# Two fused transformer layers on one core: loads of the first layer regrouped, the second layer's first weights loaded during the first layer's last batch, merged mask products and new step tables

## What is computed

```python
x = L0_attn_x                                     # [16, 512, 128]
xn = _layernorm(x)
x = x + attn0(xn) + soft_moe(xn)
xn = _layernorm(x)
x = x + attn1(xn) + routed_moe(xn)
# attn0: 16 heads; q = xn @ W_q (8 a head), c_kv = xn @ W_kv_down, k, v = c_kv @ W_k_up, c_kv @ W_v_up (8 a head),
#        one rotary part of 32 for all heads, causal softmax, @ W_o
# soft_moe: slots normed by rms, logits = norm(xn) . slots; softmax over tokens (dispatch) and over the
#        8*64 slots (combine); per expert gelu(slots @ w1 + b1) @ w2 + b2
# attn1: 16 heads of 64, keys and values from a latent of 128, causal softmax, @ w_out
# routed_moe: sigmoid scores of 16 experts, the top 8 by score + bias, normed and scaled;
#        silu(x w_gate) * (x w_up), w_down, and one shared expert
```

## Time and profile before

| | value |
|---|---|
| median of 3 runs | 3098.85 us (3097.3 to 3101.01) |
| the profiled execution | 3096.49 us, span 3094.8 us |
| mean granted PE clock | 0.984 |
| PE busy | 2884.3 us (93%) in 23492 matmuls |
| DVE / ACT / POOL busy | 2310.2 (75%) / 1802.6 (58%) / 1314.4 (42%) us |

### The profile page before, as it was taken

How to read it: one execution, slowest core, us unless ns; L and a number is a source line. 1 busy time by engine, 2 the same in 40 slices (tenths; PEclk the granted TensorE clock), 3 DMA queues, 4 the chain that set the end, 5 groups by cost and what they waited for, 6 DMA issues and landing times.

```text
span 3094.8 us, 63911 instructions
## 1 busy us (share of the span) xinstructions
PE 2884.3 (93%) x23492; PEld 1512.2 (49%) x23492; DVE 2310.2 (75%) x4199; ACT 1802.6 (58%) x3771; POOL 1314.4 (42%) x1223
## 2 busy tenths in 40 slices
PE   3999999999999984999999999999999999999997
PEld 1555555555555551444444444444444444444443
DVE  4777777777777755778878878878778778778874
ACT  2777766667776763555555555555555555555543
POOL 0433333333333321544544554554554554544543
PEclk8999999999999996999999999999999999999998
DMA  4222222222222214444444444444444444444442
GB/s 112 59 57 54 53 72 68 54 59 56 59 52 61 68 29 131 117 119 115 120 122 116 120 122 115 121 121 115 123 119 116 122 120 115 126 117 115 118 120 69
DMA packets 271910, 297.70 MB, mean 96 GB/s; under 512 B 30832, under 2 KB 235760, under 8 KB 271088
## 3 DMA queue, kind: packets, MB, share of 16 engines
q1 hardware_dynamic: 249936, 276.88, 35.2%
q10 hardware_dynamic: 21664, 16.73, 1.7%
HBM read 141.46 MB, written 25.69 MB: 54 GB/s over the span
## 4 chain that ended last, share of the span: by engine, by line
PE 51%; DMA 3%; DVE 3%; issue 2%; SPq 2%; ACT 1%; POOL 0%; DVEq 0%; ACTq 0%; POOLq 0%
PE l_ps_out L1643 8%; PE l_ps_any L1543 6%; PE l_ps_any L1545 6%; PE l_ps_any L1544 6%; PE l_ps_any L1668 5%; PE l_ps_exp L1626 4%; PE l_ps_any L1675 4%; PE l_ps_exp L1628 4%; PE l_ps_any L1601 3%; DMA l_y_rec<-rec_scratch 2%; PE l_ps_sum L1654 2%; PE l_ps_exp L1630 2%; SPq L1173 1%; DVE l_neg_max L1466 1%; PE l_ps_any L1606 1%
## 5 line engine op out<-in xcount | busy, mean ns | idle before, releaser
L1260 POOL TENSOR_TENSOR l_hid<-l_hid,l_spread 128x512 f32<-128x512 f32 x256 | 327.9, 1281 | 655.1 <-DVE l_hid L1495 480.3
L1347 ACT ACTIVATE l_probs<-l_ps_exp 128x512 f32<-128x512 f32 x640 | 376.8, 595 | 211.4 <-PE l_ps_exp L1630 201.0
L673 DVE TENSOR_REDUCE neg_max<-ps_any 128x1 f32<-128x384 f32 (+3 forms) x704 | 411.0, 634 | 115.7 <-PE ps_any L800 113.7
L536 ACT ACTIVATE probs<-ps_exp 128x512 f32<-128x512 f32 x640 | 352.1, 607 | 41.5 <-PE ps_exp L815 28.4
L455 POOL TENSOR_SCALAR_AFFINE_SELECT probs<-probs 128x512 f32<-128x512 f32 x256 | 160.0, 637 | 458.9 <-ACT probs L536 457.4
L1466 DVE TENSOR_REDUCE l_neg_max<-l_ps_any 128x2 f32<-128x768 f32 (+2 forms) x384 | 316.1, 862 | 35.4 <-PE l_ps_any L1606 34.4
L1626 PE MATMUL l_ps_exp<-l_q_a,l_k_a 128*128 128x512 f16 (+3 forms) x1024 | 306.4, 300 | 10.3 <-DMA l_q_b<-l_max_row 6.5
L1643 PE MATMUL l_ps_out<-l_probs,l_v 128*64 128x512 f32 (+3 forms) x2048 | 303.9, 439 | 0.7 <-ACT l_yT L1322 0.7
L1499 DVE TENSOR_TENSOR l_hw<-l_hid,l_hw 128x512 f16<-128x512 f32 x272 | 257.9, 953 | 60.2 <-ACT l_hw L1330 60.0
L1353 ACT ACTIVATE l_hid<-l_ps_any 128x512 f32<-128x512 f32 x272 | 162.4, 597 | 236.3 <-PE l_ps_any L1545 217.9
L1628 PE MATMUL l_ps_exp<-l_q_b,l_k_b 65*128 65x512 f16 (+3 forms) x1024 | 295.2, 300 | 0.0
(11 more groups left out here) (262 smaller groups left out, 6731.5 us busy)
## 6 DMA issues: line engine op xcount, KB each, us to landing
l_spread<-route_scratch SPq DMA_DIRECT2D x128, 512.0 KB, 4.7
l_q_a<-l_q_hi SPq DMA_DIRECT2D x256, 128.0 KB, 2.4
l_y_rec<-rec_scratch SPq DMA_DIRECT2D x128, 256.0 KB, 4.3
l_q_b<-l_q_lo SPq DMA_DIRECT2D x128, 128.0 KB, 2.4
l_k_a<-l_k_hi SPq DMA_DIRECT2D x128, 128.0 KB, 3.2
l_k_a<-l_k_lo SPq DMA_DIRECT2D x128, 128.0 KB, 2.8
l_k_b<-l_k_hi SPq DMA_DIRECT2D x128, 128.0 KB, 2.9
q_st<-rot_hi SPq DMA_DIRECT2D x64, 128.0 KB
```

The costliest lines, as they stand in the source:

```text
L536: nc.scalar.activation(probs[:, n % 2, u], ps_exp[:, (10 * g + u) % 3], ACT.Exp, scale=float(HD0 + DR) ** -0.5).then_inc(exp_done.sem, 1)
L673: nc.vector.tensor_reduce(neg_max[:, n % 2, heads[0]:heads[0] + k, t], src, AX.X, ALU.max, negate=True).then_inc(drained["dve"], 1)
L1260: nc.gpsimd.tensor_tensor(at, at, spread[:, c % 3, n % SPREAD], ALU.mult).then_inc(weighted.sem, 1)
L1347: nc.scalar.activation(probs[:, n % 2, u], ps_exp[:, (5 * p + u) % ST_BANKS], ACT.Exp, scale=float(HD1) ** -0.5).then_inc(exp_done.sem, 1)
```

## The change

Seven things are changed.

1. x of batch 0 is SP's first DMA. Of the 18 loads 8 stay with SP; the six of the rotary weights, `gamma`, the slot embeddings, `slot_gamma` and `w_o` go to ACT, ahead of w1, b1 and w2; the eight b2 go to SP, behind `load_heads(0, 2)`.
2. The norm of the slots becomes a step `snT` of the program, eight steps ahead of the first logits. The casts of the masks follow the first `scale`; `v_aug` is cleared by POOL instead of DVE.
3. A class `Early` keeps buffers that both layers share. Fourteen loads of layer 1 (masks, w_kv_down, gate, bias, w_q, w_kv_up, w_gate) are issued by ACT, one before each exponential of the last 14 of batch 15. SP loads layer 1's first x after `load_heads(15, 3)`.
4. ACT no longer waits for the last store; layer 1's loads of x wait for their own batch's.
5. At the start of layer 1, DVE norms x first and then makes the low parts, w_g's ahead of the route; w_u and w_d are cast just ahead of the first expert product and the first `hw`. PE waits for one weight at a time.
6. The mask products of a unit are merged: one of `exp` for all blocks (640 in place of 1024), one for each half and side of `max` (1280 in place of 2048).
7. Both tables are written anew, with the same steps in another order.

```diff
-    ("exp", 0, 0, 4), ("logits_s", 0, 0), ("exp", 0, 0, 5), ("exp", 0, 0, 6), ("soft_s", 0, 0),
...
+    ("exp", 0, 0, 1), ("attnT", -1, 0), ("exp", 0, 0, 2), ("max", 0, 1, 5), ("exp", 0, 0, 3), ("max", 0, 1, 6),
...
-    return [x for x in steps if 0 <= x[1] < batches]
+    steps = [x for x in steps if 0 <= x[1] < batches]
+    first = min(steps.index(x) for x in (("logits_s", 0, 0), ("logits_c", 0, 0)))
+    return steps[:first - 8] + [("snT", 0, 0)] + steps[first - 8:]
...
+        loads = [(ident[:], a["ident"]), (w_kvd[:], a["L0_attn_W_kv_down"]), (w_q[:], a["L0_attn_W_q"]),
+                 (w_k[:], a["L0_attn_W_k_up"]), (cos[:], a["cos"]), (sin[:], a["sin"]), (w_v[:], a["L0_attn_W_v_up"]),
+                 (mask[:], a["mask"])]
+        act_loads = rope + [
+            (gamma[:], a["L0_ffn_norm_gamma"].partition_broadcast(P)),
+            (slot_nat[:], a["L0_ffn_slot_embeds"].rearrange("e s d -> (e s) d").rearrange("(m p) d -> p m d", p=P)),
+            (slot_gamma[:], a["L0_ffn_slot_norm_gamma"].partition_broadcast(P)), (w_o[:], a["L0_attn_W_o"])]
...
+            sp.dma_start(x_in[:], a["L0_attn_x"][0].rearrange("(t p) d -> p t d", p=P)).then_inc(x_loaded.sem, 16)
             for dst, src in loads:
                 sp.dma_start(dst, src).then_inc(loaded, 16)
...
+                if name == "load_heads" and (b, n) == (0, 2):
+                    for dst, src in b2_loads:
+                        sp.dma_start(dst, src).then_inc(late_loaded, 16)
+                if name == "load_heads" and (b, n) == (batches - 1, G - 1):
+                    sp.wait_ge(stored.sem, stored.at(0, 16))
+                    sp.dma_start(early.x_in[:], x1_dram[0].rearrange("(t p) d -> p t d", p=P)
+                                 ).then_inc(early.x_loaded.sem, 16)
...
+            nc.gpsimd.memset(v_aug[:], 0.0).then_inc(prep_pool, 1)
+            pool.wait_ge(prep_pool, 2)
+            nc.gpsimd.memset(v_aug[:, :, :, HD0:HD0 + 1], 1.0).then_inc(prep_pool, 1)
...
+            for dst, src in act_loads:
+                act.dma_start(dst, src).then_inc(act_loaded, 16)
             act.dma_start(w1_in, a["L0_ffn_w1"].rearrange("e d h -> d e h")).then_inc(w1_loaded, 16)
             for dst, src in late_loads:
                 act.dma_start(dst, src).then_inc(late_loaded, 16)
-            act.wait_ge(prep_pe, 1)
-            nc.scalar.activation(snT[:, 0], ps_any[:, 0], ACT.Copy).then_inc(prep_act, 1)
-            act.wait_ge(prep, 13)
-            act.wait_ge(loaded, all_loaded)
...
                     act.wait_ge(exp_full.sem, exp_full.at(g, u + 1))
+                    k = len(early.loads) - (G - n) * len(EXP0) + u if b == batches - 1 else -1
+                    if k >= 0:
+                        act.dma_start(*early.loads[k]).then_inc(early.loaded, 16)
                     nc.scalar.activation(probs[:, n % 2, u], ps_exp[:, (10 * g + u) % 3], ACT.Exp,
                                          scale=float(HD0 + DR) ** -0.5).then_inc(exp_done.sem, 1)
...
                     act.dma_start(x1_dram[b].rearrange("(t p) d -> p t d", p=P), x1[:]).then_inc(stored.sem, 16)
-            act.wait_ge(stored.sem, stored.at(batches, 0))
...
-    ("v", 0, 2, 0), ("rec", -1, 1), ("sums", -1, 7), ("exp", 0, 0, 4), ("v", 0, 3, 0), ("exp", 0, 1, 0),
...
+    ("exp", 0, 0, 4), ("max", 0, 1, 2), ("exp", 0, 1, 0), ("exp", 0, 1, 1), ("v", 0, 2, 0), ("v", 0, 3, 0),
...
+            high_weights(split_in[:4])
...
                 if at == first_expert:
-                    act.wait_ge(late_loaded, all_late)
-                    for w, src in split_late:
-                        nc.scalar.activation(w[:, 0], src, ACT.Copy, scale=W_SCALE).then_inc(weights_hi, 1)
-                    act.wait_ge(weights_lo, len(split_in) + len(split_late))
+                    act.wait_ge(up_loaded, 32)
+                    high_weights(split_late[:1])
+                if at == first_hw:
+                    act.wait_ge(down_loaded, 32)
+                    high_weights(split_late[1:])
+                    act.wait_ge(weights_lo, len(split_in) + 1)
+                if name == "xnT" and b == 0:
+                    high_weights(split_in[4:])
+                if name == "exp" and (b, n, step[3]) == (0, 0, 0):
+                    act.wait_ge(weights_lo, len(split_in))
...
-            low_weights(split_in, 0)
...
                 if at == first_expert:
-                    low_weights(split_late, len(split_in))
+                    low_weights(split_late[:1], len(split_in))
+                if at == first_hw:
+                    low_weights(split_late[1:], len(split_in) + 1)
...
+                if name == "scale" and b == 0:
+                    dve.wait_ge(early.loaded, early.all)
+                    low_weights(split_in[:3], 0)
                 if name == "scale":
                     dve.wait_ge(rstd_ok.sem, rstd_ok.at(b, 1))
                     nc.vector.scalar_tensor_tensor(out=shift[:], in0=mv[:, :, 0], scalar=-1.0, in1=rstd[:],
                                                    op0=ALU.mult, op1=ALU.mult).then_inc(stats_ok.sem, 1)
+                if name == "xnT" and b == 0:
+                    low_weights(split_in[3:4], 3)
+                    casts()
+                if name == "gate" and b == 0:
+                    low_weights(split_in[4:], 4)
...
                 if at == first_expert:
-                    pe.wait_ge(weights_lo, len(split_in) + len(split_late))
-                    pe.wait_ge(late_loaded, all_late)
+                    pe.wait_ge(weights_lo, len(split_in))
+                if name == "up_in" and step[1:] == (0, 0):
+                    pe.wait_ge(weights_lo, len(split_in) + 1)
+                if name == "down" and step[1:] == (0, 0):
+                    pe.wait_ge(weights_lo, len(split_in) + 2)
...
+                if name == "max" and step[1:] == (0, 0, 0):
+                    pe.wait_ge(prep, 14)
+                    pe.wait_ge(prep_pool, 2)
+                    pe.wait_ge(weights_lo, len(split_in))
...
-                    for q, t, c in MAX1[step[3]]:
+                    for k, (q, t, c) in enumerate(MAX1[step[3]]):
                         w = (t + 1) * P
                         for r, rows in sides:
                             pe.matmul(scores[r][:, c:c + w], q_hi[rows, q, t * P:t * P + P], k_hi[rows, q, 0:w],
-                                      start=True, stop=False)
-                        for half in range(2):
-                            to = c + t * P + HD1 * half
-                            for r, rows in sides:
-                                ins = pe.matmul(scores[r][:, to:to + HD1], later_h[rows, half], ident_2[rows],
-                                                start=False, stop=(half == 1))
+                                      start=(k == 0), stop=False)
+                    blocks = diagonals([c + t * P for q, t, c in MAX1[step[3]]])
+                    for half in range(2):
+                        for r in range(2):
+                            rows = slice(HD1 * r, HD1 * r + HD1)
+                            out = scores[r].rearrange("p (x h k) -> p x h k", h=2, k=HD1)[:, blocks, half]
+                            ins = pe.matmul(out, later_h[rows, half], ident_2[rows, 0:len(MAX1[step[3]])],
+                                            start=False, stop=(half == 1))
...
-                                  start=True, stop=False)
+                                  start=(c == 0), stop=False)
-                        ins = pe.matmul(out[:, 0:P], ident_h[:], mask_h[:], start=False, stop=True)
-                    ins.then_inc(exp_full.sem, 1)
+                    out = ps_exp[:, m % ST_BANKS].rearrange("p (x q) -> p x q", q=P)
+                    pe.matmul(out[:, diagonals([c for r, k, c in EXP1[step[3]]])], ident_h[:],
+                              mask_h[:, 0:len(EXP1[step[3]])], start=False, stop=True
+                              ).then_inc(exp_full.sem, 1)
...
+class Early:
+        self.stage = ctx.enter_context(nc.sbuf_tensor("stage", [P, STAGE], F32))
+        self.ident = ctx.enter_context(nc.sbuf_tensor("ident", [P, P], F32))
+        self.bias = ctx.enter_context(nc.sbuf_tensor("l1_bias", [P, E1], F32))
+        self.loaded = ctx.enter_context(nc.semaphore("early_loaded"))
+        self.x_in = ctx.enter_context(nc.sbuf_tensor("l1_x_in", [P, TB, D], F32))
+        self.x_loaded = Count(ctx, nc, "l1_x_loaded", 16)
+        self.stored = Count(ctx, nc, "l0_stored", 16)
+        self.loads = [(masks[HD1 * r:HD1 * r + HD1, half], a["maskT"][HD1 * half:HD1 * half + HD1])
+                      for r in range(2) for half in range(2)]
+        self.loads += [(masks[:, 2], a["maskT"]), (w_kvd, a["L1_attn_w_kv_down"]), (gate, a["L1_ffn_gate_w"]),
+                       (self.bias[:], a["L1_ffn_expert_bias"].partition_broadcast(P)), (w_q, a["L1_attn_w_q"])]
+        self.loads += [(w_kvu[:, k:k + H * HD1], of[:, k:k + H * HD1]) for k in (0, H * HD1)]
+        of = a["L1_ffn_w_gate"]
```

(26 more changed lines are left out.)

334 lines of the change are left out of this document (171 added, 163 removed).

## The result

The changed kernel takes 3156.57 us (median of 4 runs, 3151.89 to 3161.88) against 3098.76 us: a ratio of 1.0186, 95% interval 1.0169 to 1.0204. It is 58 us slower where 46 us less were forecast.

A forecast was written before the change was run, and what follows sets the result against it. PE's own work was taken to bound both layers, leaving its idle time to win. -13 - 18.1 - 18.7 + 3.3 = -46.5 on 3096.5 gives 3050; the runs' median, 2.4 us above, gives 3052, range 3024 to 3080.

The forecast's parts named there:

- The start, -13: Start of layer 0: x loaded first lets PE begin sooner, first score product at 28 to 34 us; -13 us (8 to 19).
- 22 - 3.5 = 18.5: Start: ACT's copy of `xnT` 22 us earlier, less 3.5 for q and k's way through DRAM while w1 and w2 arrive.
- The slots' wait: Start: PE waits in full at `snT` for the slots' norm, some 5.5 us given back.
- The crossing, -18: From layer 0 to layer 1: PE's first instruction comes 21.1 us earlier; with give-backs -18.1 us, between -12 and -24.
- my 7: First expert product of layer 1: 7 of the 9.7 us wait remain in pieces, from w_u and w_d's casts; -2.7 us.
- ACT's fourteen issues: Batch 15 of layer 0: fourteen DMA issues ahead of ACT's exponentials, about 0.45 us each, cost +3.5 us.
- Layer 0's order, -19: Layer 0's new table: half of PE's 28.4 us waits on `y_un`, `xn`, `disp_s` go (-14), plus -4.7 from tiling; -18.7 us.
- the 49 changes of tiling: Layer 0: 49 fewer switches of PE between full-array and part-array products, some 0.1 us each; -4.7 us.
- Merged masks, -2: Layer 1's exponential units: two mask products of 0.06 us become one of 0.11, 384 times; about 2 us less.
- Layer 1, +3: Layer 1: tiling changes +5.3, merged masks -2, waits under the new order 0 (between -15 and +20); +3.3 us.
- The +5.3 for 56 more changes of tiling: Layer 1: 56 more switches of PE between full-array and part-array products, some 0.1 us each; +5.3 us.
- The rival that decided: Layer 1's order costs more than all loads win, through a new wait each batch; 3113 us at 4 us a batch; chance 0.04.

## Why the prediction was wrong

- **The start, -13.** The first product comes 18.1 us earlier, where 22 - 3.5 = 18.5 were forecast, at 34.49, just past my 28 to 34; ACT's copy at 13.74 is inside its range. The slots' wait is 4.34 where I had 5.5. The 3.46 us at the second row of maxima, with b2's eight loads (5.01 us on SP) ahead of it, were not in my sum, though they were in the diff, and neither was the slower clock that follows. Right in mechanism; the size holds up to the first product.
- **The crossing, -18.** PE's first instruction comes 22.9 us earlier against the store, where I had 21.1. The wait ahead of it is 8.87 in place of 31.80. The casts of w_u and w_d leave waits of 2.97 and 5.37 us, near my 7; the profile puts the second down to `l_neg_max`, which DVE makes behind w_d's low part (3.15 us from 1184.50). What ACT's fourteen issues cost no run shows. Right in mechanism and, as far as it can be seen, in size.
- **Layer 0's order, -19: wrong too.** The mechanism was half seen. The waits on `xn` and `y_un` went as I said; I took the one on `disp_s` to shrink with them and did not ask what becomes late next: POOL's masking, and the heads' loads. Nothing is left, with or without the 49 changes of tiling, whose -4.7 I can't find in either pair of runs.
- **Merged masks, -2.** Between -1 and -7.
- **Layer 1, +3: the step that failed.** I wrote that "the new table takes some away and makes new ones" and "I take 0, between -15 and +20". It costs 95 to 102 us: 71 of waits for the row of maxima and 30 of the lower clock. I had looked at how short the waits are in the earlier trace rows, which says how little there is to win and nothing of how much there is to lose. The view held a row for `l_q_b<-l_max_row`, 6.5 us, 5 times, and I did not put it among my rows: a transfer that PE already waits for now and then has little slack. I compared the tables by PE's steps and by DVE's, not by what SP's queue has ahead of the row and what holds it. And I put nothing into the sum for what a wait does to the clock. The +5.3 for 56 more changes of tiling isn't seen: with `rec_in(-1,2)` moved, PE's products take 1836.5 us against 1837.6 with the old table. Reading the 0.16 us of the earlier trace rows as 0.1 us a change was not borne out in either layer.
- **The rival that decided** had 0.04. I did name the sum from which it turns, 3.1 us a batch; the waits came to 71/16 = 4.5 us, and with the clock to 6.4. I named DVE's maxima and a head's loads as its place, and the place was the row of maxima in SP's queue.
- **Luck.** With `rec_in(-1,2)` moved the time is 3067.11, within my range for the wrong reason. With layer 1's table taken back it is 3055.65, near my 3052, and that too is partly luck: the terms without layer 1's order add up to -13 - 18.1 - 18.7 - 2 = -51.8, and 38 us were won; what is missing is about layer 0's order.
